# Expert 0's first block narrowed to 64 columns, and the rest of expert 0 gathered by one-hot products

## The reference

```
h   = einsum('eth,efh->etf', layernorm(x), ctx); g = gelu(h)
x   = x + tanh(g_xattn) * einsum('etf,efh->eth', g, ctx)      # "attention" without softmax
xf  = layernorm(x).reshape(896, 256)
top1 = argmax(xf @ gate_w.T + gate_b)
out = for every token: relu(xf @ w1[top1].T + b1[top1]) @ w2[top1].T + b2[top1]
x   = x + tanh(g_ffn) * out
```

## Time and profile before

| | |
|---|---|
| median of 3 runs | 110.49 us (110.0 to 111.1) |
| the profiled execution | 110.59 us, span 108.8 us |
| PE busy | 98.6 us, 91% of the span |
| weight loads (PEld) busy | 90.4 us, 83% |
| DVE, ACT, POOL busy | 53.5, 31.9, 40.0 us |
| granted TensorE clock | full in all slices but the last |
| the chain that ended last | PE 66%, DVE 12%, DMA 7%, POOL 5% |

### The profile page before, as it was taken

How to read it: one execution, slowest core, us unless ns; L and a number is a source line. 1 busy time by engine, 2 the same in 40 slices (tenths; PEclk the granted TensorE clock), 3 DMA queues, 4 the chain that set the end, 5 groups by cost and what they waited for, 6 DMA issues and landing times.

```text
span 108.8 us, 2102 instructions
## 1 busy us (share of the span) xinstructions
PE 98.6 (91%) x676; PEld 90.4 (83%) x677; DVE 53.5 (49%) x206; ACT 31.9 (29%) x98; POOL 40.0 (37%) x97
## 2 busy tenths in 40 slices
PE   5997999998996995999999999999999999999800
PEld 5986888887876893999999899899998998998600
DVE  0362787598588783898623324153223250433010
ACT  5616355554351440332304123023041230220000
POOL 3268687335376647702403473030030120300330
PEclk9999999999999999999999999999999999999998
DMA  3999999999995103699999999999991010010100
GB/s 76 328 378 395 423 431 419 410 422 405 394 420 199 54 0 98 172 382 358 397 405 401 428 405 370 418 424 428 425 409 68 6 44 0 0 40 6 48 23 31
DMA packets 6799, 28.66 MB, mean 264 GB/s; under 512 B 1150, under 2 KB 2560, under 8 KB 4737
## 3 DMA queue, kind: packets, MB, share of 16 engines
q1 hardware_dynamic: 4752, 25.40, 58.2%
q0 software_dynamic: 864, 2.12, 6.4%
q10 hardware_dynamic: 1168, 0.98, 2.8%
HBM read 26.64 MB, written 2.11 MB: 264 GB/s over the span
## 4 chain that ended last, share of the span: by engine, by line
PE 66%; DVE 12%; DMA 7%; POOL 5%; issue 4%; SPq 1%; ACT 1%; POOLq 0%; DVEq 0%
PE bank L996 26%; PE bank L1005 26%; PE bank L946 6%; PE bank L935 4%; DMA x<-in_x 4%; DMA region<-x_rows,from_row 3%; DVE x L593 2%; PE bank L978 2%; DVE stats L609 2%; DVE cand L642 1%; DVE lg L632 1%; PE bank L925 1%; POOL mv L290 1%; POOL out_rows L388 1%; DVE first L647 1%
## 5 line engine op out<-in xcount | busy, mean ns | idle before, releaser
L996 PE MATMUL bank<-region,w 128*128 128x128 f32 x288 | 34.8, 277 | 0.9 <-ACT region L493 0.9
L996 PEld LDWEIGHTS bank<-region,w 128*128 128x128 f32 x288 | 33.8, 192 | 1.4 <-ACT region L493 0.9
L1005 PE MATMUL bank<-w,region 128*128 128x256 f32 x144 | 32.6, 380 | 0.0
L1005 PEld LDWEIGHTS bank<-w,region 128*128 128x128 f32 x144 | 26.7, 191 | 3.2
L529 ACT ACTIVATE region<-bank,smalls 128x128 f32<-128x128 f32 x40 | 12.5, 363 | 40.0 <-PE bank L996 40.0
L388 POOL DMA_INDIRECT out_rows<-region,to_row x9 | 8.9, 988 | 34.6 <-DVE region L838 33.2
L822 DVE TENSOR_SCALAR region<-bank,smalls 128x128 f32<-128x128 f32 x32 | 9.6, 346 | 13.6 <-PE bank L996 13.0
L383 POOL DMA_INDIRECT region<-x_rows,from_row x9 | 9.4, 1046 | 15.3 <-DMA region<-x_rows,from_row 12.0
L838 DVE SCALAR_TENSOR_TENSOR region<-bank,tg,region 128x256 f32<-128x256 f32 (+1 forms) x9 | 4.4, 484 | 20.9 <-PE bank L1005 20.9
L935 PEld LDWEIGHTS bank<-w,region 128*128 128x128 f32 x96 | 11.8, 192 | 1.0 <-DVE w L584 0.2
L946 PE MATMUL bank<-region,w 128*112 128x272 f32 x48 | 12.4, 394 | 0.0
(11 more groups left out here) (119 smaller groups left out, 81.7 us busy)
## 6 DMA issues: line engine op xcount, KB each, us to landing
w<-in_w1t SPq DMA_DIRECT2D x8, 1024.0 KB, 21.0
w<-in_w2t SPq DMA_DIRECT2D x8, 1024.0 KB, 23.0
region<-in_ctx SPq DMA_DIRECT2D x5, 792.0 KB, 11.7
region<-in_ctx SPq DMA_DIRECT2D x3, 408.0 KB, 7.2
region<-in_ctx SPq DMA_DIRECT2D x3, 384.0 KB, 4.4
x_rows<-x ACTq DMA_DIRECT2D x8, 113.8 KB, 6.5
b2b<-in_b SPq DMA_DIRECT2D x1, 896.0 KB, 12.0
x<-in_x_rest SPq DMA_DIRECT2D x1, 670.0 KB, 6.1
```

The costliest lines, as they stand in the source:

```text
L996: mm = pe.matmul(hT_ps[k][:, part % 2 * P:(part % 2 + 1) * P], w1[:, e, n * H + part * P:n * H + (part + 1) * P], xgT[:, j % 2, n * P:(n + ...
L1005: mm = pe.matmul(y[:, 0:D], hidT[:, q, part, :], w2[:, e, part * D:(part + 1) * D], start=(part == 0), stop=(part == KH - 1))
```

## The change

Block 0 becomes 64 columns wide (`SMALL_BLOCK`). Its gather (`gather_small`, 6 products of 64 columns) is placed in front of the attention products of batch 7. `up_small` has 16 products of 64 columns with the same weights as before. `down_small` computes the transposed result: the 128x128 pieces of w2 are the weights and 64 columns stream (16 products instead of 8 with 256 columns); ACT copies it (`yT`) and `turn_small` (2 products) transposes it back, after `up(1)`. Tokens of the early batches beyond 64 are given ranks from 128 on (`move_far`), which puts them in an overflow block.

Block 1 (expert 0, batches 3 to 7) is no longer gathered from HBM for its products: `gather_first(b)` does it by 2 one-hot products of 128 columns for each of five batches. Its rows are still fetched for the residual, third in the order of gathers, which is now 2, 0, 1, 3. The normalised rows `xn2` of all batches are kept, so DVE has five more `norm_x2`, and POOL and DVE make five more one-hot matrices (`pick_expert_0`).

The batches are routed as 3, 1, 2, 2 (before 3, 1, 1, 1, 1, 1). `route(0, 3, 1)` moves on DVE from behind `add_attention(3)` to before it, and `rank_sums(0, 3)` on PE from behind `scores(6)` to behind `attend(4)`. `rank_sums` of later batches stand behind all attention. The third batch's statistics (`of_x(2)`) move on POOL ahead of the constants. SP holds the weights of experts 2 to 6 until block 1's one-hot products are done and block 2's gather has landed.

```diff
-MAX_OVER = CHUNKS - 1
+MAX_OVER = CHUNKS
+SMALL_BLOCK = 64
...
-        xn2 = w2[:, E - 1, 0:EARLY * D].rearrange("p (b n) -> p b n", b=EARLY)
+        yT = w1[:, E - 1, 2 * CC * S:2 * CC * S + KD * SMALL_BLOCK]
+        pick_s = w1[:, E - 1, H:H + EARLY * SMALL_BLOCK].rearrange("p (b n) -> p b n", b=EARLY)
...
         xn = w1[:, E - 2, 0:B * D].rearrange("p (b n) -> p b n", b=B)
+        xn2 = xn
...
@@ sync
             sp.wait_ge(xnT_done, B)
-            sp.wait_ge(xgT_done, 1)
-            sp.wait_ge(first_in[1], 16)
+            sp.wait_ge(xgT_done, 2)
             sp.wait_ge(xg_in[0], 16)
             load_expert(2)
             sp.dma_start(b2b[:, D:E * D], b2[D:E * D].partition_broadcast(P)).then_inc(b2_in[1], 16)
-            for e in range(3, E):
+            for e in range(3, E - 1):
                 load_expert(e)
+            sp.wait_ge(y_done, 1)
+            load_expert(E - 1)
@@ gpsimd
+            of_x(2)
+            std_of_x(2)
...
             of_x2(4)
+            pick(0, 1)
+            pick(1, 1)
             running_count(4)
-            pick(0, 1)
+            pick(2, 1)
             of_x2(5)
-            pick(1, 1)
-            pick(2, 1)
             running_count(5)
             running_count(6)
+            place()
             of_x2(6)
             of_x2(7)
-            pick(3, 2)
-            pick(4, 2)
-            running_count(7)
-            place()
-            pick(5, 3)
+            for b in range(EARLY, 6):
+                pick_expert_0(b)
+            for b in range(EARLY, 6):
+                pick(b, 2)
...
-            for j in (1, 2, 0, *range(3, BLOCKS)):
+            for j in (2, 0, 1, *range(3, BLOCKS)):
@@ scalar
                 if b == B - 2:
-                    expert_0()
+                    pick_early()
+                if b == B - 1:
+                    small_copy()
+                x_share(b)
                 if b >= 1:
                     store_x2(b - 1)
-                if b == B - 1:
-                    first_halves()
+            small_relu(0)
+            small_relu(1)
             store_x2(B - 1)
+            small_relu(2)
+            small_relu(3)
+            yT_copy()
+            first_halves()
@@ vector
             for b in range(B):
                 if b == 6:
-                    route(5, 1, 4)
+                    route(4, 2, 3)
                 add_attention(b)
                 stats_x2(b)
                 join_x2(b)
-                if 1 <= b <= EARLY:
+                if 1 <= b <= 5:
                     norm_x2(b - 1)
...
-                if b == 3:
-                    dve.wait_ge(consts_ok, 12)
+                if b == 2:
+                    dve.wait_ge(consts_ok, 13)
                     route(0, 3, 1)
-                    is_expert_0()
                 if b == 4:
+                    own_count(0, 3, 1)
+                    rank_of(0, 3, 1, rank0_ok)
+                    move_far()
                     route(3, 1, 2)
-                    own_count(0, 3, 1)
-                    rank_of(0, 3, 1)
...
+            norm_x2(5)
+            own_count(3, 3, 2)
+            rank_of(3, 3, 2, rank_ok)
+            norm_x2(6)
+            route(6, 2, 4)
+            norm_x2(7)
+            own_count(6, 2, 3)
+            rank_of(6, 2, 3, rank_ok)
+            for b in (6, 7):
+                pick_expert_0(b)
+            for b in (6, 7):
+                pick(b)
+            place(6, 2)
@@ tensor
+            def gather_small():
+                for k in range(KD):
+                    for b in range(EARLY):
+                        pe.wait_ge(pick_s_ok, b + 1)
+                        pe.wait_ge(xn2_ok, b + 1)
+                        mm = pe.matmul(xs_ps[:, k * SMALL_BLOCK:(k + 1) * SMALL_BLOCK], xn2[0:S, b, k * P:(k + 1) * P],
+                                       pick_s[0:S, b, :], start=(b == 0), stop=(b == EARLY - 1))
+                mm.then_inc(xgT_done, 1)
+            def gather_first(b):
+                pe.wait_ge(xn2_ok, b + 1)
+                for k in range(KD):
+                    mm = pe.matmul(x1_ps[k][:, 0:P], xn2[0:S, b, k * P:(k + 1) * P], pick_x[0:S, b - EARLY, :],
+                                   start=(b == EARLY), stop=(b == B - 1))
...
+            def up_small():
...
+                        mm = pe.matmul(hTs_ps[part // 2][:, part % 2 * SMALL_BLOCK:(part % 2 + 1) * SMALL_BLOCK],
+                                       w1[:, 0, n * H + part * P:n * H + (part + 1) * P],
+                                       xgT[:, 0, n * SMALL_BLOCK:(n + 1) * SMALL_BLOCK], start=(n == 0), stop=(n == KD - 1))
...
+            def down_small(k):
+                for part in range(KH):
...
+                    mm = pe.matmul(yT_ps[:, k * SMALL_BLOCK:(k + 1) * SMALL_BLOCK],
+                                   w2[:, 0, part * D + k * P:part * D + (k + 1) * P], hidT[:, 0, part, 0:SMALL_BLOCK],
+                                   start=(part == 0), stop=(part == KH - 1))
...
             for b in range(B):
                 if b + 1 < B:
                     scores(b + 1)
-                if b == 5:
-                    pe.wait_ge(consts_ok, 12)
-                    rank_sums(0, 3)
                 if b + 2 < B:
                     turn_xn(b + 2)
+                if b == B - 1:
+                    gather_small()
                 attend(b)
-                if b == 6:
-                    pe.wait_ge(oh_ok, 3)
-                    rank_sums(3, 2)
-
-            first_half(0).then_inc(half_done, 1)
-            first_half(1).then_inc(xgT_done, 1)
...
+                if b == 4:
+                    pe.wait_ge(consts_ok, 13)
+                    pe.wait_ge(oh_ok, 1)
+                    rank_sums(0, 3)
+
...
+            pe.wait_ge(oh_ok, 3)
+            rank_sums(3, 3)
+            up_small()
+            pe.wait_ge(pick_mid_ok, 1)
+            pe.wait_ge(x2_ok, B)
+            gather_first(3)
+            pe.wait_ge(rank_read, 2)
+            pe.wait_ge(w2_in[0], 16)
+            down_small(0)
...
+            down_small(1)
...
+            gather_first(4)
...
+            gather_first(7)
...
-            up(0, range(5, KH))
-            pe.wait_ge(w2_in[0], 16)
-            down(0, 0, 0, range(0, KH - 2))
-            turn_block(1, 1)
-            down(0, 0, 0, range(KH - 2, KH))
-            up(1, range(0, KH - 2))
+            up(1)
+            turn_small()
+            down(1, 1, 0, range(0, KH - 2))
             turn_block(2, 0)
-            up(1, range(KH - 2, KH))
+            down(1, 1, 0, range(KH - 2, KH))
             up(2, range(0, KH // 2))
...
-            up(2, range(KH // 2, KH))
+            up(2, range(KH // 2, KH - 2))
+            turn_block(3, 1)
+            up(2, range(KH - 2, KH))
```

More of the change, by code:

```diff
@@ L354, in _ @@
             pool.memset(cum[:, 0, :], 0.0).then_inc(consts_ok, 1)
-            for b in range(2, 6):
+            pool.memset(cnt_add[:], 0.0).then_inc(pool_step, 1)
+            pool.wait_ge(pool_step, 8)
+            pool.memset(cnt_add[:, 0:1], float(P - SMALL_BLOCK)).then_inc(consts_ok, 1)
+            for b in range(3, 6):
                 of_x(b)
@@ L530, in relu @@
                                        bias=b1[:, bass.ds(e * KH + 2 * k + r, 1)]).then_inc((hTa_ok, hTd_ok)[k % 2], 1)
-            relu(0, 0, 0, later=False, pairs=range(4))
-            xgT_copy(1, 1)
-            relu(1, 1, 0, later=False)
+            relu(1, 1, 0, later=False, pairs=range(4))
             xgT_copy(2, 0)
@@ new lines, in pick_expert_0, with place @@
+            def pick_expert_0(b):
+                dve.wait_ge(rank_ok, 3)
+                dve.wait_ge(is_e0_ok, 4)
+                dve.tensor_scalar(pick_x[0:S, b - EARLY, :], iota_r[0:S, :], rank[0:S, b:b + 1], is_e0[0:S, b:b + 1],
+                                  ALU.is_equal, ALU.mult).then_inc(pick_end_ok, 1)
+            def place(b, n):
+                dve.wait_ge(oh_ok, 4)
+                dve.tensor_tensor(pick_e0[0:S, b:b + n, :], oh[0:S, b:b + n, :],
+                                  idw[0:S, b:b + n].unsqueeze(2).to_broadcast([S, n, C]),
+                                  ALU.mult).then_inc(place_last_ok, 1)
@@ L962, in rank_sums @@
                 same_batch(b, n, start=False, stop=True).then_inc(rk_done, 1)
-            def first_half(k):
-                for b in range(EARLY):
-                    pe.wait_ge(pick_x_ok, b + 1)
-                    mm = pe.matmul(xg0_ps[k][:, 0:P], xn2[0:S, b, k * P:(k + 1) * P], pick_x[0:S, b, :],
-                                   start=(b == 0), stop=(b == EARLY - 1))
-                return mm
+            def gather_small():
[6 more added lines that the diff above has]
+                mm.then_inc(xgT_done, 1)
@@ new lines, in down_small @@
+            def down_small(k):
+                for part in range(KH):
+                    if k == 0:
+                        pe.wait_ge((hTa_ok, hTd_ok)[part // 2 % 2], part // 4 * 2 + part % 2 + 1)
+                    mm = pe.matmul(yT_ps[:, k * SMALL_BLOCK:(k + 1) * SMALL_BLOCK],
```

(46 more changed lines are left out.)

200 lines of the change are left out of this document (97 added, 103 removed).

## The result

| | before | after |
|---|---|---|
| median, us | 110.64 (110.0 to 111.1, 4 runs) | 116.28 (116.26 to 116.6, 4 runs) |
| ratio | | 1.0521 [1.0463, 1.0579] |
| profiled execution, us | 110.59, span 108.8 | 116.26, span 114.5 |
| PE's last product ends | 103.03 | 108.75 |
| mean granted clock | 0.995 | 0.981 |

The change costs 5.6 us, and PE's end moves by 5.72. The forecast was 114.4, with 115.9 as its upper end: the sign was right, the size was not.

What follows compares the result with a forecast made beforehand. PE was taken to bound the second stage, so PE's work and waits, added and removed, were summed: +3.9 us on the profiled 110.6, less 0.1, gave 114.4 us. The range was 111.2 to 115.9.

Steps and rivals of the forecast that it cites:

- start: Batch 2's deviation ahead of POOL's constants removes PE's wait before batch 2's transpose: -0.58 us.
- wait for the rank sums: PE, behind batch 4's attention, waits 2.4 us for POOL's second running count, where it waited 0.40: +2.0 us.
- block 1's one-hot products: 10 added products on PE, 20 records at 0.112 us each: +2.2 us.
- three waits gone: PE's waits for block 0's copy (0.85), last one-hot matrices (0.18) and block 1's HBM rows (1.18) go: -2.2 us.
- small rank and count products: Three groups instead of five save small waits between dependent products on PE: -0.4 us (0 to -0.8).
- block 3's gather: New PE wait before block 3's transpose, its rows delayed by weights on the DMA engines: +2.5 us (0 to 3.7).
- clock: The sum had no term for PE's clock falling; only a rival priced that.
- rival 4: PE's clock falls to the 1.2 GHz level in the two long waits: +1 to +4, so 115.5 to 118.5; chance 0.06.
- 1 (gather in time): Block 3's gather lands unloaded, 8.9 us behind the table, so its wait goes: 111.9 us; chance 0.14.
- 2: 64-column records cost 0.056 us less each over 76 records; with block 3's wait 111.3 us, no change; chance 0.10.
- 3: Columns set the pace, the faster table frees DVE and POOL, block 3's wait is covered: 108.4 to 109.0; chance 0.07.
- 5: The overflow block runs; excluded by the token counts, no chance given.

Runs made afterwards that it cites:

- e2_warm: Changed kernel with 16 unused products of the identity with itself on PE before block 3's transpose: 114.55 us, ratio 1.0374.
- e6_early: Kernel before the change, with only batch 2's deviation put ahead of POOL's constants: 110.33 us, ratio 0.9997.
- e1_hold: Changed kernel with expert 2's weights loaded right behind expert 1's and all others held until block 3's gather landed: 110.92 us, ratio 1.0044.
- e4_wide: Changed kernel with block 0 at 128 columns instead of 64, same order of work: 117.12 us, ratio 1.054.
- e5_both: Changed kernel with e1_hold's edit and the rank sums of batches 0 to 2 back behind batch 6's scores: 109.62 us, ratio 0.9923.

## Why the prediction was wrong

| step of the sum | predicted | measured | where |
|---|---|---|---|
| start | -0.58 | -0.1 | attention 4 ends 22.61 + 1.54 = 24.15, before 24.23 |
| wait for the rank sums | +2.0 | +1.0 | 1.42 against 0.40 |
| small gather | +0.3 | +0.2 | 33.08 - 31.55 = 1.53 against 1.34 |
| `down_small` | +0.1 | +0.1 | 1.73 + 1.84 = 3.57 against 3.46 |
| block 1's one-hot products | +2.2 | +2.3 | 0.50 + 1.84 |
| three waits gone | -2.2 | -2.2 | no brackets |
| small rank and count products | -0.4 | some -0.9 | below |
| block 3's gather | +2.5 | +3.9 | 3.88 |
| clock | 0 | +1.4 | 0.25 + 1.18; the 0.22 of a pair behind a wait was there before too |
| sum | +3.9 | +5.7 | PE's end: +5.72 |

**The first step that failed is the clock.** It cost 1.4 us. The sum put it at nothing, and rival 4, with its +1 to +4, had a chance of 0.06. The prediction itself forecast two waits longer than any inside the span before and then priced the records behind them as if the clock did not see them. The measured time lies in that rival's 115.5 to 118.5. e2_warm shows this cost apart from the wait (1.4 us by its rows, 1.6 by the ratios).

**The second, as large, is the size of block 3's wait:** 3.88 us against 2.5. The mechanism was right in its parts: released by the first gather (4.4 us after the table, 4.8 forecast), PE early (10.8, 10.6 forecast), gather caught by the weights. But its flight was kept at the 6.8 us of before with an allowance for one more gather; it took 8.7. The sum took 2.5 between 0 and 3.7, nearer to "only the place changed" than to "a gather more in front". A gather more in front it was, and it made the flight 2.0 us longer where the bound of 3.7 has 1.5, so the upper end, slightly passed, was the right value. The two errors are one event: a wait of 3.88 us, and what the clock did in it.

**Two errors went the other way, one did not.** The rank sums came at 25.58, not 26.0, and PE was there at 24.16, not 23.6. The first count begins at 24.9, as forecast (24.95); but from there to the rank sums the forecast kept 1.08 us, and it took 0.67, with all three counts in one row of 0.91 us:

```profile
24.36 0.55 POOL L302 TENSOR_TENSOR x<-x,power 112x1 f32<-112x1 f32 x1
24.87 0.91 POOL L337 TENSOR_TENSOR cum<-cum,oh 112x9 bf16<-112x9 bf16 x3
```

That the count is held by batch 3's statistics was right: batch 3's deviation is the first of these rows. PE's 0.58 at the start was not to be had (e6_early), since another wait stood 4 us behind it; this added 0.5 to the miss. And the small products were worth 0.5 more than forecast. The row that ended them before is, in PE's order of time of the kernel before:

```profile
39.45 2.76 PE L1005 MATMUL bank<-w,region 128*128 128x256 f32 x12
```

From 34.43 to 39.45, 5.02 us, less 32 x 0.112 of `up` and 0.18 of waiting, leaves 1.26 us of small products between the pieces of block 0; those between 34.56 and the table's last product now take some 0.5, and the two-batch group at 30.44, 0.13 us, is gone.

The forecast missed by only 1.9 us because the rank sums and the small products hid 1.5 us of its other errors, which is luck.

**The signs.** Of those set out as right, only `up_small` in 3.6 us came true. The rank sums' wait (1.42, not 2.0 to 2.8), block 3's (3.88, not 1.5 to 3.6), the table (44.60, not 45 to 46) and PE's end (108.75, not near 107) all missed.

**The rivals.** 1 (gather in time) did not happen, but e1_hold makes it so: 110.92, a us under the 111.9 it was given, for the wait of the rank sums was over-sized by that much. 2 and 3 (columns set the pace) fall with 3.62 us for 32 records and with e4_wide; the load rows 0.11 apart were the right evidence. 4 happened, on top of the forecast, not instead of it. 5 did not.

**Where the 5.6 us come from, in sum:** block 3's gather under the weights, 5.3 us with the clock (e1_hold; the clock alone 1.4 to 1.6 by e2_warm), and the rank sums, 1.3 (e5_both against e1_hold). Without both the change is worth -0.8%. Block 1's extra products are paid by the waits they fill.

## What to carry to other kernels

Where a change moves work so that the same wait ends sooner on one side, ask which transfers the earlier release sets off and what is queued behind them. Here a release 1.3 us earlier after the table put two gathers under a stream of weights, while PE came 3.6 us sooner for the rows. One expert's load ahead of the gathers, with the rest held until the last urgent one had landed, took back 5.3 of the 5.6 us. A forecast wait of PE that is longer than any in the trace must be priced twice, once as idle time and once as the slower records behind it; the second price varied here between executions. And for float32 with a weight load in front of every record, count products, not columns, up to 128 columns; with 256 a record took 0.216 us instead of 0.112.
